# One block of edge counts kept on chip between two phases, shares per block, and 512-column products in the graph convolutions

## Time and profile before

| | us |
|---|---|
| median of 3 runs | 2115.71 |
| lowest, highest | 2114.61, 2118.65 |
| profiled execution, its own time | 2117.84 |
| span of its trace | 2115.9 |

### The profile page before, as it was taken

One profiled execution on the slowest core, in us unless ns is written; L12 is line 12 of the kernel. 1 busy time (PEld: TensorE's weight loads), 2 busy tenths in 40 slices (PEclk: granted clock), 3 DMA queues, 4 the chain that ended last, 5 costly groups with the idle time before them and its releaser, 6 DMA issues. The chain is left out here.

```text
span 2115.9 us, 42215 instructions
## 1 busy us (share of the span) xinstructions
PE 1749.2 (83%) x13965; PEld 1581.7 (75%) x13965; DVE 1278.1 (60%) x2275; ACT 1139.2 (54%) x1914; POOL 100.7 (5%) x124
## 2 busy tenths in 40 slices
PE   0346777728898988886999969999999999997997
PEld 0235666628888888885666659999999999995785
DVE  3767888828988889896343452222331223447897
ACT  0004777738787778784333345555666565652322
POOL 2531111100000000000000000000000000000000
PEclk9866887859999999998899989999999999997998
DMA  8221555557303030301000054444454444530102
GB/s 180 33 44 43 160 160 160 160 152 139 88 13 88 13 88 13 88 1 29 0 0 0 0 121 111 111 106 127 126 132 119 118 104 119 130 97 25 30 0 61
DMA packets 142784, 173.97 MB, mean 82 GB/s; under 512 B 27412, under 2 KB 134319, under 8 KB 142541
## 3 DMA queue, kind: packets, MB, share of 16 engines
q1 hardware_dynamic: 136858, 163.51, 30.4%
q0 software_dynamic: 5808, 8.86, 2.0%
HBM read 126.24 MB, written 46.04 MB: 81 GB/s over the span
## 5 line engine op out<-in xcount | busy, mean ns | idle before, releaser
L1453 PE MATMUL ps_sets<-arena,kinds 125*125 125x195 bf16 x5000 | 451.0, 251 | 89.8 <-DVE kinds L1382 82.2
L1453 PEld LDWEIGHTS ps_sets<-arena,kinds 125*125 125x125 bf16 x5000 | 437.7, 138 | 103.2 <-DVE kinds L1382 51.5
L2031 ACT ACTIVATE onewide<-onering 125x625 fp32r (+1 forms) x500 | 361.1, 727 | 252.9 <-PE oneps L1861 250.4
L1349 ACT ACTIVATE kinds<-ed_rows,es_mask 125x625 bf16<-125x625 f32 x500 | 366.2, 808 | 110.6 <-PE ps_sets L1453 81.1
L1861 PE MATMUL oneps<-oneparts_a,onewide 125*125 125x258 f32 x2500 | 307.5, 285 | 18.4 <-ACT onewide L2031 18.4
L1861 PEld LDWEIGHTS oneps<-oneparts_a,onewide 125*125 125x125 f32 x2500 | 303.3, 188 | 19.9 <-issue 18.7
L1861 PE MATMUL oneps<-oneparts_b,onewide 125*125 125x258 f32 x2500 | 301.8, 283 | 0.0
L1861 PEld LDWEIGHTS oneps<-oneparts_b,onewide 125*125 125x125 f32 x2500 | 300.2, 187 | 0.7
L1380 DVE TENSOR_TENSOR kinds<-kinds,cnt_block 125x2500 bf16<-125x2500 bf16 x120 | 182.4, 1520 | 72.3 <-ACT kinds L1349 63.2
L1922 DVE COPY oneraw<-oneps 125x257 f32<-125x257 f32 x100 | 35.1, 419 | 311.0 <-PE oneps L1861 311.0
L1382 DVE TENSOR_TENSOR kinds<-cnt_block,kinds 125x2500 bf16<-125x2500 bf16 x120 | 182.2, 1519 | 8.9
(11 more groups left out here) (262 smaller groups left out, 1826.9 us busy)
## 6 DMA issues: line engine op xcount, KB each, us to landing
onering<-counts SPq DMA_DIRECT2D x50, 683.6 KB
onering<-countsT SPq DMA_DIRECT2D x50, 683.6 KB
countsT<-tr SPq DMA_DIRECT2D x25, 683.6 KB
counts<-blk SPq DMA_DIRECT2D x5, 3418.0 KB
cnt_block<-counts SPq DMA_DIRECT2D x25, 546.9 KB
ed_rows<-ed_dram SPq DMA_DIRECT2D x20, 273.4 KB
onering<-counts SPq DMA_DIRECT2D x50, 79.3 KB
onering<-countsT SPq DMA_DIRECT2D x50, 79.3 KB
```

The source lines that it names most:

```text
L1349: a.activation(kinds[:, slots(m)[0] + s, 0, :], ed_b[:, h, :], ACT.Relu, scale=MASK_SCALE, bias=k.es_mask[:, t0 + s, h:h + 1]).then_inc(ma ...
L1453: last = t_.matmul(ps[0:P, BANK[h % 2][u], e * W3:(e + 1) * W3], kinds[:, slots(m)[0] + s, e, u * P:(u + 1) * P], parts[:, t, h, e, :, :]. ...
L2031: a.activation(wide[:, t % RF, :], ring[:, bass.ds((i * NS + (NS * U * n + s)) % RB, 1), w, :] .rearrange("p a d -> p (a d)"), ACT.Copy).t ...
```

## The change

1. `count_phase`: the loops over tiles are split by blocks j (`for j in range(U)`, with tile 0 of each written out and a loop over the four others), so that the double buffer is two tensors: `k.blk`, which lives on into the attention, for even j, and `blk_odd`. SyncE starts the phase with a load of the last block's `ed` rows, all heads (`k.ed_b`, 1.2 MB written), and no longer waits for the stores of `counts` at its end.
2. `gat_separable_phase`: the order of blocks is 4, 0, 1, 2, 3 (`data(b)`). The first finds counts and `ed` rows on chip; X is loaded at once; the others are loaded as before. `add_parts` becomes two adds; the maximum, the reciprocal and the product are made once for each block for four heads (`shares`), as is the addition to X; the statistics move ahead of group 4 of head 1.
3. `convolutions_phase`: a row is kept as low, high, ones. Step 0 keeps its two matmuls (258 and 256 columns); steps 1 to 3 make one matmul of 512 columns. The degrees are kept from step 0 (column of ones, and for the rows `accum_out` of ScalarE's copies, summed by `row_degrees`). VectorE applies the share straight from PSUM, two instructions for each `kk`, and frees the bank after the second. In the first and last fifth of a block the banks go in two turns, 0 to 2 and 3 to 4.

```diff
 count_phase
-        blk = sb("blk", [P, 2, T, QB], BF16)
+        blk = [k.blk, sb("blk_odd", [P, T, QB], BF16)]
-                with act.Fori(1, T) as i:
-                    act.wait_ge(blk_stored, 32 * (i // U + 1))
+                for j in range(U):
+                    act.wait_ge(blk_stored, 32 * (j + 1))
+                    tile(j, 0)
+                    with act.Fori(1, U) as w:
+                        tile(j, w)
 (TensorE alike; SyncE:)
+                for lo_, hi_ in SPLIT:
+                    sp.dma_start(k.ed_b[lo_:hi_, :, :],
+                                 k.ed_dram[:, (U - 1) * U:T, :]....to_broadcast([hi_ - lo_, HEADS, QB])).then_inc(k.ed_first, 16)
-                sp.wait_ge(blk_stored, 32 * U + 64)
                 sp.wait_ge(tr_stored, 32 * T + 64)
 gat_separable_phase
-        cnt = sb("cnt_block", [P, T, QB], BF16)
-        ed_b = sb("ed_rows", [P, HEADS, QB], FP32)
+        cnt, ed_b = k.blk, k.ed_b
+        def data(b):
+            return (b + U - 1) % U
-                load_ed(0, 0)
-                for m in range(NM):
-                    load_cnt(0, m)
-                    ...
                 (load of X)
+                sp.wait_ge(k.blk_stored, 32 * U + 64)
 (ScalarE, block 0:)
-                        act.wait_ge(ed_in[h], 32 * (j + 1))
+                            act.wait_ge(k.ed_first, 32)
-                def add_parts():
-                    v.tensor_reduce(out=num[:, :, :], in_=both...."p u (c d) -> p u d c", op=ALU.add)
-                    (drain, maximum, drain, reciprocal, drain)
+                def add_parts(h):
+                    v.tensor_tensor(out=num[:, h, :, :], in0=both[:, :, 0:D1], in1=both[:, :, D1:2 * D1], op=ALU.add)
+                    v.drain()
+                    v.tensor_tensor(out=num[:, h, :, :], in0=num[:, h, :, :], in1=both[:, :, 2 * D1:W3], op=ALU.add)
+                    v.drain()
+                def shares():
+                    v.tensor_scalar(den, num[:, :, :, DH:D1], 1e-16, None, ALU.max)      # 20 elements
+                    v.reciprocal(den, den)
+                    v.tensor_tensor(out=num[:, :, :, 0:DH], in0=num[:, :, :, 0:DH], in1=den.to_broadcast(...), op=ALU.mult)   # 1280
+                def add_to_x(b):
+                    v.tensor_tensor(out=x, in0=x, in1=num[:, :, :, 0:DH], op=ALU.add)    # 1280
+                            if not first:
+                                if m == 4 and h == 0: shares()
+                                if m == 5 and h == 0: add_to_x(b - 1)
+                                if m == 4 and h == 1: batch_stats(..., data(b - 1))
 convolutions_phase, TensorE
+                        turns = [(0, 1, 2), (3, 4)] if s in (0, NS - 1) else [range(U)]
+                        for some in turns:
+                            for w in range(U):
+                                (wait for the wide tile, if some[0] == 0)
+                                for kk in some:
+                                    (wait c_out, if t == 0)
+                                    if n == 0:
+                                        t_.matmul(ps[0:P, kk, 0:FD], tile, rows[:, t % T, F:X2], ...)
+                                        last = t_.matmul(ps[0:P, kk, 0:F], tile, rows[:, t % T, 0:F], ...)
+                                    else:
+                                        last = t_.matmul(ps[0:P, kk, :], tile, rows[:, t % T, 0:2 * F], ...)
+                                if some[-1] == U - 1:
+                                    last.then_inc(wide_used, 1)
 VectorE, means_out, n = 1 and 3 (n = 2: tensor_scalar, then the same)
+                            v.scalar_tensor_tensor(out=raw[:, kk, 0:F], in0=lo, scalar=share, in1=bias[:, n // 2, :], ...)
+                            v.drain()
+                            v.scalar_tensor_tensor(out=full[:, kk, :], in0=hi, scalar=share, in1=raw[:, kk, 0:F], ...).then_inc(c_out, 1)
 ScalarE, n = 0
+                                a.activation(wide[...], tile, ACT.Copy, accum_out=row_sums[...]).then_inc(wide_done, 1)
```

More of the change, by code:

```diff
@@ L781, in _ @@
                 sp.sem_inc(z_read, 1)
[L782 removed]
+                for lo_, hi_ in SPLIT:
+                    sp.dma_start(k.ed_b[lo_:hi_, :, :],
+                                 k.ed_dram[:, (U - 1) * U:T, :].rearrange("h t p -> h (t p)").unsqueeze(0).to_broadcast([hi_ - lo_, HEADS, QB]))\
+                        .then_inc(k.ed_first, 16)
+                for j in range(U):
                     with sp.Fori(0, U) as w:
@@ L1350, in masks, with block_masks @@
                                      bias=k.es_mask[:, t0 + s, h:h + 1]).then_inc(mask_done, 1)
-                def block_masks(j, first):
+                def block_masks(b, first):
                     for h in range(HEADS):
-                        before = None if first and h == 0 else (j, h - 1) if h else (j - 1, HEADS - 1)
+                        before = None if first and h == 0 else (b, h - 1) if h else (b - 1, HEADS - 1)
                         for m in range(NM):
@@ L1409, in block_kinds @@
+                def block_kinds(b, first):
                     for h in range(HEADS):
-                        before = None if first and h == 0 else (j, h - 1) if h else (j - 1, HEADS - 1)
+                        before = None if first and h == 0 else (b, h - 1) if h else (b - 1, HEADS - 1)
                         for m in range(NM):
@@ L1931, in means_out @@
-                    v.drain()
-                    for kk in range(U):
-                        if n % 2 == 0:
-                            v.tensor_scalar(tmp[:, kk, :], raw[:, kk, 0:F], inv[:, kk:kk + 1], None, ALU.mult)
-                        else:
-                            v.scalar_tensor_tensor(out=full[:, kk, :], in0=raw[:, kk, 0:F], scalar=inv[:, kk:kk + 1], in1=bias[:, n // 2, :],
-                                                   op0=ALU.mult, op1=ALU.add)
+                        hi, lo = ps[0:P, kk, F:2 * F], ps[0:P, kk, 0:F]
@@ L1939, in means_out @@
+                    if n == 0:
+                        v.drain()
+                        v.tensor_copy(degree[:, 0:U], raw[:, :, F])
+                        v.drain()
+                        inverse(inv[:, 0, bass.ds(i * U, U)], U)
+                        for kk in range(U):
+                            v.tensor_scalar(tmp[:, kk, :], raw[:, kk, 0:F], inv[:, 0, bass.ds(i * U + kk, 1)], None, ALU.mult)
                     v.drain()
```

283 lines of the change are left out of this document (160 added, 123 removed).

## The result

The changed kernel takes 2092.08 us (median of 4 runs, 2086.63 to 2096.32) against 2115.16 us before, a ratio of 0.989 with an interval of 0.9858 to 0.9922. It is faster by 1.1%, 23 us where 72 were forecast, and its time lies just above the range. Its profiled execution took 2089.4 us. The table holds the two traces against each other, from start to start of the matmuls that it names (the difference of the spans, 2115.9 - 2087.8, is 28.1 us). Of the forecast's 45 us for the convolutions, 1.3 lay behind their last matmul and stand in the last row.

The account below looks back on a forecast made before the run. TensorE was taken to bound the convolutions, TensorE and VectorE near balance the attention. Gains 15.3 - 2 + 14 + 45 = 72.4 us off the profiled 2117.8 gave 2045.4, 2043 on the median; 8-in-10 range 2029 to 2090.

Parts of the forecast that it names:

- Part 3: Convolutions: a 512-column product at 215.9 ns replaces a 240.8 ns pair, 46.7 us gained; 45 us with the smaller terms.
- the columns set the price: Rival, 19%: one wide matmul costs as two, so the convolutions give nothing and the time is 2088 us.
- The wait for a bank: Convolutions: TensorE waits for VectorE to free bank 2, some 0.3 us in each of ten blocks; 3 us lost, bounds 0 and 15.
- Part 1: Way into the attention: the waits for the counts store and the `ed` row go; 15.3 us gained, bounds 5.2 and 15.4.
- the wait does not go: Rival, 10%, combines: stores of `countsT` are waited for as late as those of `counts`; 10 us less gained, 2053.
- The `ed` load: Start of the count phase: 1.2 MB loaded beside the first `z`, for which VectorE waits; 2 us lost, bounds 0 and 3.3.
- Splitting the loops: Count phase, TensorE and ScalarE: costed at nothing; upper bound 15 us if entering the ten new bodies stalled TensorE.
- Part 2: Attention: shorter `add_parts`, with shares and the add to X once a block; 14 us gained, bounds 6 and 28.
- Heads 2: Attention, mid-block heads: 24.10 us falls to 22.6, 1.5 gained; bounds 0.8 and 2.4.
- block 0: Attention's first block, without `shares`: three heads at 1.5 us and 0.9 for its waits on counts, 5.4 gained.
- Head 1: Attention, second head of a block: the moved statistics make a 2.3 us gap; loses 0.7 us against now.
- the gaps only move: Rival, 20%, combines: TensorE may run slow behind a new attention gap, 1.5 us each time; attention gives 6, time 2051.

Follow-up runs that it names:

- c_fp32: Changed kernel with each wide product of the last three convolution steps split into two of 256 columns, operands read as plain fp32: 3272.7 us.
- c_quarter: Changed kernel with each wide product of the last three convolution steps split into four of 128 columns, each with its own weight load: 2476.24 us.
- t_store: Changed kernel with the store of the last block of counts issued behind the branch, at the head of the attention's SyncE queue: 2080.6 us, ratio 0.983.
- b_all: b_pool with the addition to X cut in two pieces and the batch statistics in five, placed between groups: 2070.88 us, ratio 0.9767.
- a_old: Changed kernel with the old shares, five additions to X after each head and the statistics' old place: 2097.49 us, ratio 0.9908.
- b_pool: t_store with the load of the `ed` rows on GpSimd's queue, between the first load of z and the loop: 2078.9 us, ratio 0.9812.
- c_zero: Changed kernel with the wide products of the last three convolution steps reading zeros from one tile in place of the rows: 2086.92 us.
- c_same: Changed kernel with the wide products of the last three convolution steps reading the first tile of rows each time: 2089.55 us.

## Why the prediction was wrong

**Part 3 is the step that failed: 45 us forecast, 13.6 measured (12.7 up to the last matmul, 0.9 behind it).** I took 215.9 ns as the price of a wide product, because the nearest row showed what I counted as 512 cycles, 2.6 ns above the bare ones. The row is right, the transfer from it is not. It shows one of the two records of a product (c_fp32), 256 columns in 215.9 ns, and so a TensorE that takes in a column every 0.84 ns. Both rows in which I found no surcharge are near that rate: this one, and the half clock of the earlier trace rows with 0.83 (214 ns for 257). The row at about twice the rate, 0.468 ns a column, had one: 120.4 ns for 257 columns, 13.3 above the estimate of 107.1. That was read as one fixed cost for each matmul, the weight load, that a wide product would pay half as often and hide. Measured, a matmul takes 119.1 ns at 256 columns and 232.8 at 512: between these two, 0.444 ns a column and 5.4 fixed. Only the 5.4 is saved by widening, and 0.9 by the two columns of ones that went: 6.3 ns a product (240.8 - 234.5) instead of 24.9. What c_quarter met, the load or not, is 109 ns, below the 119. In the traces the three steps took 11.9 us less (483.0 before, 471.1 after), where the forecast had 46.7. The rival "the columns set the price" came nearest, at 0.468 ns a column and nothing gained, 2088 us; it had a fifth of the chance and should have had most of it. That the result lies near its 2088 is in part luck, since Parts 1 and 2, which it kept whole, fell short by 12 us.
The wait for a bank came about as forecast. In the block that begins at 1524.4, VectorE is done with bank 2 at 1524.88 (1524.40 + 0.48), TensorE's first product for it starts at 1524.94, and this start and the next are 333 ns behind the one before instead of 233: 0.2 us in each of 14 blocks, 2.8 us, where I had 0.3 in ten. In step 0 little changed (172.7 us for 173.4).

**Part 1 was right in what goes, short by a cost that was not in any row: 15.3 forecast, 10.6 measured.** `countsT` did land early (SyncE goes on at 454.8 in after, right behind the store's issue; 449.8 in t_store), so the rival "the wait does not go" is out. But before, the wait for the store had left the DMA engines idle when the branch fetched its code. Taking the wait away put that fetch behind the store: ScalarE's 8.3 us from branch to masks, where t_store has 3.4, are the missing 4.7 and a little more. The `ed` load cost 3.2 in the first tile (12.1 us, 8.9 before), near the upper bound of 3.3, where I took 2. Splitting the loops cost nothing: tiles of 9.9 us as before.

**Part 2: 14 forecast, 6.6 measured.** Heads 2 have 22.6 us, to the tenth what I worked out; block 0 gained 2.7 where 5.4 stood, since its last head with the back-edge took 0.8 more, where 1.5 less was forecast. Head 0 gained by little, as forecast. Head 1 was to lose 0.7 and loses 0.9 at the full clock (25.06) and 2.4 to 2.6 in three blocks of four, in which TensorE runs slow behind the gap. How often it does is chance as far as the traces show (one of four in t_store, with the same code there). That is the rival "the gaps only move", with its 1.5 us; it had 20%. Its cure, shown by b_all, is to cut the work, not to make it less. Head 3 with the back-edge differs from block to block by 0.9 us in a_old and by 3.1 in b_all, with the other kernels between, and no run was made to find out why.

**The sum.** For the profiled execution the forecast was 2045.4 and the result 2089.4, 44.0 off: 31.0 are the convolutions, 4.7 the way into the attention, 7.4 the attention and its end, 1.2 the count phase, 0.4 the last stretch, less 0.7 that came by chance in the first. The median is 49 off because the profiled execution of before lies above its median and that of after 2.7 below.

## What to carry to other kernels

Before a duration is taken from another line's row, count its records against the code's products, and compare the rate at which data go in: a row at half the rate says nothing of a limit at the full one (here 0.84 ns a column, and 0.45 to 0.47 for the products it was to price). A wait that is taken away also kept the transfers behind it apart (here TensorE's branch went from 4.3 us to 8.2); look at what is fetched or loaded next, code included, and put big stores behind a branch. And where an engine runs a few groups ahead of another, once-a-block work cost by its longest piece here (b_all, cut in pieces, has 486.3 us of attention for b_pool's 496.9): cut it between groups before making it cheaper.

## What the runs showed that I had not expected

- At a granted clock of 1.00, fp32r matmuls take 119.1 ns at 256 columns and 232.8 at 512, 0.444 ns for each column between, not the estimated 0.417. With bf16 operands, of which one width was run, 512 columns take 227.7 ns, 14 above the bare 213.3. The records of plain fp32 products, 256 columns each, are 215.9 to 216.1 ns apart, 2.6 to 2.8 above 213.3, what 512 columns would take by that estimate. Neither zeros nor one place (233.0 ns each), nor sums of one product (232.8), nor a short weight load (232.4) change the 232.8. In after the spacing doesn't follow the DMA traffic beside it (232.8 ns in the quietest quarter of the three steps, 232.7 in the busiest); in c_zero and c_same the busiest quarter is 2 to 3 ns longer, far from the 19.5. The cause stays open.
- A plain fp32 product of 256 columns appears as two records 216 ns apart, each with a weight load of 187 ns (c_fp32).
- Matmuls of 128 columns with a weight load each follow at 109.2 ns, though the load's record is 189 ns long (c_quarter).
- TensorE's branch into the attention took 4.3 us with the DMA queues near idle and 8.2 behind a 3.8 MB store (t_store and after); ScalarE's, up to its next instruction, 3.4 and 8.3.
